# Selective scan with a quantized feed-forward: dt u B of two states and D u by diagonal products on TensorE, state 11's C product on GpSimd

## What is computed

```python
dA = jnp.exp(d[..., None] * A)                              # d is dt, per channel and position
state = state * dA + (d * u)[..., None] * b[:, None, :]     # 16 states per channel
y = jnp.einsum('bdn,bn->bd', state, c)
...
y = (y + D[None, :, None] * x) * silu(z)
...
x = x + jnp.tanh(g_xattn[0]) * xattn(ctx, layernorm(x), ...)
x = x + jnp.tanh(g_ffn[0]) * ffn(layernorm(x), w_gate, w_up, w_down)
```

## Time and profile before

| | |
|---|---|
| median of 3 runs | 623.98 us (623.07 to 625.08) |
| the profiled execution | 624.87 us |
| its span, first to last instruction | 623.1 us |
| mean granted clock of TensorE | 0.970; 1.00 in the windows of units 5 to 15 |

### The profile page before, as it was taken

The page is one execution under the profiler, slowest core; times in us unless marked ns, Lnnn a source line. Parts: engine busy times, 40 slices in busy tenths (PEclk is TensorE's granted clock), DMA queues, the critical chain, the costliest instruction groups (busy, mean ns, idle before and its releaser), DMA issues. The chain is left out here.

```text
span 623.1 us, 9210 instructions
## 1 busy us (share of the span) xinstructions
PE 501.2 (80%) x3014; PEld 338.2 (54%) x3014; DVE 564.6 (91%) x777; ACT 510.7 (82%) x761; POOL 519.9 (83%) x286
## 2 busy tenths in 40 slices
PE   6999666856576788888768888888697978899997
PEld 2443355745575665556555655555465655555553
DVE  2899979999999999999999999999999999987564
ACT  3869789886997898969598989786889898778784
POOL 1568799999999999999999999999999999941000
PEclk9999768789889999999999999999999999999999
DMA  8992941710751010118400111075101010000001
GB/s 284 400 413 80 347 157 34 262 60 1 283 184 40 1 51 2 34 35 312 163 34 35 35 34 35 34 265 207 37 34 35 35 34 19 1 17 18 18 18 50
DMA packets 29985, 64.47 MB, mean 103 GB/s; under 512 B 3681, under 2 KB 11873, under 8 KB 26866
## 3 DMA queue, kind: packets, MB, share of 16 engines
q1 hardware_dynamic: 29938, 63.89, 28.5%
HBM read 55.75 MB, written 8.13 MB: 103 GB/s over the span
## 5 line engine op out<-in xcount | busy, mean ns | idle before, releaser
L759 POOL TENSOR_TENSOR area_s<-area_s,b_bc 128x1024 f32<-128x1024 f32 x128 | 300.6, 2365 | 7.9 <-DMA b_bc<-bc_rows 3.6
L438 PE MATMUL pY<-ident,area_s 128*128 128x128 f32 x640 | 103.2, 287 | 79.7 <-DVE area_s L1329 76.8
L438 PEld LDWEIGHTS pY<-ident,area_s 128*128 128x128 f32 x640 | 73.3, 145 | 108.6 <-DVE area_s L1329 78.9
L1005 ACT ACTIVATE pA<-dt_all,a_neg 128x512 f32<-128x512 f32 x160 | 107.7, 681 | 13.8 <-DVE area_s L1321 12.8
L1321 DVE TENSOR_TENSOR_SCAN area_s<-pA,area_s 128x512 f32<-128x512 f32 x96 | 114.2, 1204 | 4.2 <-ACT pA L1005 3.6
L481 PE MATMUL pG<-wq_gu,area_f 128*128 128x512 fp8e4 x448 | 106.6, 379 | 3.7 <-ACT area_f L955 2.9
L751 POOL TENSOR_TENSOR u_all<-u_all 128x1024 f32<-128x1024 f32 x44 | 104.0, 2363 | 0.2 <-DMA u_all<-bc_rows 0.2
L1329 DVE TENSOR_TENSOR area_s<-area_s,pC 128x512 f32<-128x512 f32 x144 | 95.1, 663 | 2.4 <-DVE area_s L1321 0.7
L432 PE MATMUL pC<-ident,xdT 128*128 128x128 f32 x576 | 90.4, 284 | 3.1 <-DVE area_s L1329 1.9
L432 PEld LDWEIGHTS pC<-ident,xdT 128*128 128x128 f32 x576 | 69.9, 143 | 11.4 <-DVE area_s L1329 8.3
L481 PEld LDWEIGHTS pG<-wq_gu,area_f 128*128 128x128 bf16 x448 | 41.9, 98 | 48.1 <-ACT area_f L955 3.9
(11 more groups left out here) (197 smaller groups left out, 977.7 us busy)
## 6 DMA issues: line engine op xcount, KB each, us to landing
b_bc<-bc_rows SPq DMA_DIRECT2D x16, 1024.0 KB, 8.0
area_s<-x SPq DMA_DIRECT2D x32, 256.0 KB, 3.0
u_all<-bc_rows SPq DMA_DIRECT2D x14, 512.0 KB, 6.2
b_bc<-w_gate SPq DMA_DIRECT2D x1, 4096.0 KB, 14.3
dt_all<-x SPq DMA_DIRECT2D x1, 4096.0 KB, 24.6
area_f<-w_up SPq DMA_DIRECT2D x1, 4096.0 KB, 34.0
area_f<-w_down SPq DMA_DIRECT2D x1, 4096.0 KB, 15.1
out<-area_f SPq DMA_DIRECT2D x16, 256.0 KB, 2.1
```

The lines of the kernel that those rows point to most:

```text
L438: mm = pe.matmul(pY[:, k * P:(k + 1) * P], src[:, k * P:(k + 1) * P], ident[:, :], is_transpose=True, start=(first and k == 0), stop=(last ...
L759: gp.tensor_tensor(db[c % NDB], du[s % 2].rearrange("p (a l) -> p a l", a=1).to_broadcast([P, CH, L]), b_bc[:, CH * c:CH * c + CH, :], ALU ...
L1005: act.activation(exp_bank(s, n), dt_all[:, s, :], ACT.Exp, scale=a_neg[:, s % NT, n:n + 1]).then_inc(S["s_exp"], 1)
```

## The change

From unit 5 on (`PE_FROM`):

- dt u B of states 4 and 5 (`PE_PAIR = 2`) is made by PE instead of POOL. `du_transpose` transposes dt u into pT, ACT copies it to SBUF (`copy_duT`, step 15 of the unit before), and `db_state` multiplies it, as stationary operand, with 128x128 diagonal matrices of B into the PSUM bank that would have held the exponential. The exponential of these two states goes to the SBUF buffer `db[2]` instead, and the scan swaps its operands. The diagonals are made by ACT from `ident` and a column of `xdT`, eight for each batch, in the last unit of the batch before (unit 4 for the first).
- The product of state 11 with C is made by POOL alone (`times_c_alone`, 512 columns, with a row of C broadcast by a DMA), and PE sums it from there (`y_sum_alone`). DVE's product and PE's broadcast of C for this state go.

In all units D u is no longer made on ACT: ACT makes a 128x128 diagonal of D (`diag_d`), and `y_skip` multiplies u with it into pY. In units 0 to 3 it moves to an earlier step. Some small tiles move to tensors of their own. The core of the diff:

```diff
+PE_FROM = PLAIN + 1
+PE_PAIR = 2
+ALONE = 11
+def alone(s, n):
+    return s >= PE_FROM and n == ALONE
 def own(s):
-    return [n for n in range(NS) if n // CH not in pooled(s)]
+    return [n for n in range(NS) if n // CH not in pooled(s) and not alone(s, n)]
+def pool_pairs(s):
+    return [c for c in range(NCH) if s < PE_FROM or c != PE_PAIR]
+DIAGONAL_AT = {3: ((0, 0), (0, 1)), 4: ((0, 2), (0, 3)), 5: ((1, 0),), 6: ((1, 1),), 9: ((1, 2),), 10: ((1, 3),)}
+def by_pe(s, n):
+    return s >= PE_FROM and n // CH == PE_PAIR
...
+        h_alone = carve(area_f, 4096, L)
+        c_alone = carve(area_f, 7680, L)
-        du_skip = carve(area_s, 8192, L)
+        duT = carve(area_s, 8192, L).rearrange("p (k d) -> p k d", k=NT)
+        diag_b = [b_bc[:, CH * PE_PAIR + i, :].rearrange("p (k l) -> p k l", k=NT) for i in range(CH)]
...
             def load_u(s):
                 past(sp, S["s_du"], s - 1)
-                past(sp, S["s_skip"], s - 1)
+                past(sp, S["s_skd"], s - 1)
...
+            def load_c_alone(b):
+                if b == 1:
+                    sp.wait_ge(S["k_p3"], 2 * NW + 1)
+                else:
+                    sp.wait_ge(S["s_amul"], b * NT - PE_FROM)
+                sp.dma_start(c_alone, bc_rows[b, NS + ALONE].partition_broadcast(P)).then_inc(S["d_ca"], 16)
...
+                    first = 4 * q + (CH if b * NT >= PE_FROM and 2 * q == PE_PAIR else 0)
...
+            def y_sum_alone(s):
+                pe.wait_ge(S["s_amul"], s - PE_FROM + 1)
+                y_part(h_alone).then_inc(S["s_aytr"], 1)
...
             def y_skip(s):
                 if s >= PLAIN:
                     pe.wait_ge(S["s_y"], s)
+                past(pe, S[f"d_u{s % 2}"], (s // 2) * 16)
                 pe.wait_ge(S["s_skip"], s + 1)
-                y_part(du_skip, first=(s >= PLAIN)).then_inc(S["s_skd"], 1)
+                for k in range(NT):
+                    mm = pe.matmul(pY[:, k * P:(k + 1) * P], u_in[s % 2][:, k * P:(k + 1) * P], diag_d[:, :],
+                                   start=(s >= PLAIN and k == 0), stop=False, skip_group_check=True)
+                mm.then_inc(S["s_skd"], 1)
+            def du_transpose(s):
+                pe.wait_ge(S["s_du"], s + 1)
+                pe.wait_ge(S["s_szT"], s)
+                for k in range(NT):
+                    mm = pe.transpose(pT[:, k * P:(k + 1) * P], du[s % 2][:, k * P:(k + 1) * P], ident[:, :])
+                mm.then_inc(S["s_dup"], 1)
+            def db_state(s, i):
+                n = CH * PE_PAIR + i
+                pe.wait_ge(S["s_duT"], s - PE_FROM + 1)
+                pe.wait_ge(S["s_diag"], CH * NT * (s // NT - 1) + NT * (i + 1))
+                pe.wait_ge(S["s_scan"], s * NS + n - 2)
+                for k in range(NT):
+                    mm = pe.matmul(exp_bank(s, n)[:, k * P:(k + 1) * P], duT[:, k, :], diag_b[i][:, k, :], start=True, stop=True)
+                mm.then_inc(S["s_dbp"], 1)
...
             def down(t, part, z_done):
...
-                    pe.wait_ge(S["s_szT"], z_done)
+                    if z_done < UNITS:
+                        pe.wait_ge(S["s_duT"], z_done - PE_FROM + 1)
+                    else:
+                        pe.wait_ge(S["s_szT"], z_done)
...
-                    if n == NS - 1:
+                    if n == 10:
                         y_skip(s)
...
             for s in range(PLAIN, UNITS):
                 t1, t2 = s - NT, s - NT - 1
-                fill(s, 0, 1)
+                if s >= PE_FROM:
+                    du_transpose(s)
                 if s > PLAIN:
                     y_sum(s - 1, 15)
                     y_sum_pooled(s - 1, 3)
                 c_bcast(s, 2)
-                fill(s, 1, 2)
+                fill(s, 0, 1)
+                if s >= PE_FROM:
+                    db_state(s, 0)
+                    db_state(s, 1)
                 y_skip(s)
                 y_sum(s, 2)
                 c_bcast(s, 3)
-                fill(s, 2, 4)
+                fill(s, 1, 4)
...
-                    c_bcast(s, 11)
...
-                y_sum(s, 11)
+                if ALONE in own(s):
+                    y_sum(s, ALONE)
...
                     up(t1, 3)
+                    if s >= PE_FROM:
+                        y_sum_alone(s)
                     y_sum(s, 14)
...
+            def times_c_alone(s):
+                gp.wait_ge(S["d_ca"], (s // NT) * 16)
+                gp.wait_ge(S["s_scan"], s * NS + ALONE + 1)
+                gp.tensor_tensor(h_alone, h_alone, c_alone, ALU.mult).then_inc(S["s_amul"], 1)
...
                     times_b(s + 1, 1)
-                    times_b(s + 1, 2)
+                if s >= PE_FROM:
+                    times_c_alone(s)
                 times_c(s, 3)
...
             def exponential(g):
                 s, n = g // NS, g % NS
+                if by_pe(s, n):
+                    act.wait_ge(S["s_scan"], (s - 1) * NS + CH * (PE_PAIR + NDB) + CH)
+                    act.activation(db[PE_PAIR][:, n % CH, :], dt_all[:, s, :], ACT.Exp, scale=a_neg[:, s % NT, n:n + 1]).then_inc(S["s_exp"], 1)
+                    return
...
             def skip(s):
-                past(act, S[f"d_u{s % 2}"], (s // 2) * 16)
                 past(act, S["s_skd"], s)
-                act.activation(du_skip, u_in[s % 2], ACT.Copy, scale=d_raw[:, s % NT:s % NT + 1]).then_inc(S["s_skip"], 1)
+                act.activation(diag_d[:, :], ident[:, :], ACT.Copy, scale=d_raw[:, s % NT:s % NT + 1]).then_inc(S["s_skip"], 1)
+            def copy_duT(s):
+                act.wait_ge(S["s_dup"], s - PE_FROM + 1)
+                past(act, S["s_dbp"], CH * (s - PE_FROM))
+                act.activation(duT.rearrange("p k d -> p (k d)"), pT[:, :], ACT.Copy).then_inc(S["s_duT"], 1)
+            def diagonal(b, i, k):
...
+                n = CH * PE_PAIR + i
+                act.activation(diag_b[i][:, k, :], ident[:, :], ACT.Copy, scale=xdT[:, b, k, n:n + 1]).then_inc(S["s_diag"], 1)
...
+                    if s == PE_FROM - 1 and n in (2, 4, 6, 8):
+                        diagonal(1, n // 6, n - 2 - 4 * (n // 6))
+                        diagonal(1, n // 6, n - 1 - 4 * (n // 6))
+                    if s % NT == NT - 1 and s + 1 < UNITS and n in DIAGONAL_AT:
+                        for i, k in DIAGONAL_AT[n]:
+                            diagonal(s // NT + 1, i, k)
...
                     if n == 14:
                         z_copy(s)
+                    if n == 15 and s + 1 < UNITS:
+                        copy_duT(s + 1)
...
             def scan(s, n):
                 dve.wait_ge(S["s_exp"], s * NS + n + 1)
-                if n % CH == 0:
-                    dve.wait_ge(S["s_dbu"], s * NCH + n // CH + 1)
+                at, dbu = exp_bank(s, n), db[(n // CH) % NDB][:, n % CH, :]
+                if by_pe(s, n):
+                    dve.wait_ge(S["s_dbp"], CH * (s - PE_FROM) + n % CH + 1)
+                    at, dbu = dbu, at
+                elif n % CH == 0:
+                    dve.wait_ge(S["s_dbu"], db_count(s, n // CH))
...
+                elif alone(s, n):
+                    past(dve, S["s_aytr"], s - PE_FROM)
+                    h = h_alone
```

45 lines of the change are left out of this document (30 added, 15 removed).

## The result

| | before | after |
|---|---|---|
| median (runs) | 623.81 us (7, 623.07 to 625.08) | 627.99 us (7, 626.27 to 628.62) |
| the profiled execution | 624.87 us | 627.36 us |
| its span | 623.1 us | 625.5 us |

The changed kernel is slower: the ratio of the two kernels' runs is 1.0061, with a 95% interval of 1.0047 to 1.0075 (the two medians alone give 1.0067). In a later comparison it was 1.0039 (1.0018 to 1.006), with medians of 627.96 us against 624.79.

The account below looks back on a forecast made before the run. VectorE and GpSimd were taken as full, with ScalarE second bound 0.24 us behind VectorE in a loop. Terms 2.75 + 4.5 + 0.45 - 2.8 + 0.3 - 0.2 = +5.0 gave 629.0 us, range 617.5 to 634.

Parts of the forecast that it names:

- Ordinary units: Units 6, 9, 10, 13 and 14: 31.1 us each instead of 30.55, 5 x 0.55 = +2.75 us.
- unit 15: Unit 15, which issues no diagonals: +0.45 us.
- The last stretch: TensorE's last stretch loses one broadcast: -0.2 us.
- TensorE's stretch and ScalarE's chain: TensorE's 2.15 us more per unit delay copy_duT and copy_xqT; quantizing starts at 16.15 after scan 14 instead of 15.46.
- the rival of dear products: Rival, chance 0.10: fp32 products on TensorE cost 0.35 us each, +13, about 642; at 0.25, +3.4, 632.4.
- From `scale_h` to scan 14: ScalarE's quantizing of h through exponential 14: 14.9 us, putting the scan of state 14 at 31.05.
- Diagonals: Units 7 and 11: eight on ScalarE at 0.30 us, two hidden, 1.8 over 31.1 gives 32.9, +2.25 each, +4.5.
- Units 8 and 12: VectorE's 0.79 us wait goes and the saved product of 0.58 counts: 33.5 us, -1.4 each, -2.8.
- Unit 4: Unit 4 holds eight diagonals (2.4 us) among gaps of ScalarE: +0.3 us.
- TensorE fits in: Rival, chance 0.20: copy_xqT waits for ScalarE alone, ordinary units 30.5 us; -1.0 in all, 623.0.
- The relief goes through: Rival, chance 0.25: ScalarE's order has unseen room, VectorE's 0.58 us comes off each of 11 units: -6.4, 617.6.
- The two full engines' own sums: Four units (9 to 12) would need 121.2 us of GpSimd and 121.1 of VectorE, instead of 126.61.

Follow-up runs that it names:

- three moves: The changed kernel with xq's transpose ahead of nine fp8 products, all eight diagonals at step 3, and dt u transposed one unit earlier: 621.67 us, ratio 0.9941.
- the best kernel: The kernel with the three moves plus 11 idle transposes that keep TensorE busy in unit 4: 621.02 us, ratio 0.9922 against before.
- two tries to cut the loop: On the best kernel, VectorE's scales made earlier, with ScalarE's scaling half ahead of exponential 7, or both halves between exponentials 7 and 8: 623.28 and 622.91 us.

## Why the prediction was right, and where its terms were off

The predicted sign and mechanism held: from unit 4 on after is 3.3 us longer where +5.0 was the sum, and the medians differ by 4.2 in the first comparison and 3.2 in the second. Part of the closeness of 627.99 to 629.0 is luck. Ordinary units, unit 15 and units 7 and 11 were priced 3.2 us too high, unit 4 1.1 too low, and the 0.9 us between the units' 3.3 and the medians' 4.2 are not accounted for. (The last stretch, priced at -0.2, did not change: 73.14 and 73.12 us.)

**TensorE's stretch and ScalarE's chain: right to 0.2 us.** Counted from the scan of state 14: `du_transpose` at 4.61 (4.43 foreseen), `squares` 6.35 (6.25), `xq_transpose` 14.42 (14.3), `copy_xqT` 15.06 (14.97), `scale_h` 16.16 (16.15). ScalarE's wait for TensorE there is 0.57 (0.5) and VectorE's idle time ahead of scan 14 is 0.52 (0.5 or more; 0.31 in unit 6, the least). The 0.18 us of `du_transpose` are GpSimd's: its product of state 11, which was to be done at 2.9, ends at 3.18, and TensorE waits 0.30 us for it ahead of `y_sum_alone`:

```profile
366.67 0.66 PE L487 MATMUL pY<-ident,area_f 128*128 128x128 f32 x4 [0.30 <-POOL area_f L855]
```

GpSimd gained idle time as foreseen: ahead of its products for a pair it is 21.9 us over the span, where the earlier trace rows has 7.9. The price of an fp32 product is 0.22 (0.215), so the rival of dear products is out.

**From `scale_h` to scan 14: the term that was too large.** The prediction added 14.9 us. It measured 14.52 (379.59 to 394.11), so an ordinary unit came to 30.69 and not 31.1, +0.13 for +0.55, and five of them to +0.65 for +2.75. The number was read where ScalarE was abreast of VectorE, and contained the 0.34 us of waits for scans. In after, where ScalarE is the late one, they are gone: exponential 14 starts 13.79 us behind `scale_h`, for 14.16 before. The run with more work for ScalarE met the same room: its segment grew by 0.38 where 0.61 was expected. Unit 15 has the same term: +0.03 for +0.45.

**Diagonals: the cost right, the sign not.** One takes 0.295 us (0.30 foreseen). Units 7 and 11 came to 32.43 and 32.70, which is 1.7 and 2.0 over an ordinary unit where 1.8 was the sum. In the run that moved the diagonals into the hole ahead of `copy_xqT`, 1.6 of unit 7's 1.7 us and 1.7 of unit 11's 2.1 went away. But VectorE was to stand idle for over 1.5 us ahead of scan 14 there, and it is 0.79 and 1.06. The time is spread over several waits; in unit 11 the largest is one for TensorE's product of the up projection, just ahead of that scan (0.56 us before):

```profile
425.05 0.69 DVE L1404 TENSOR_TENSOR area_f<-area_f,pG 128x512 f32<-128x512 f32 x1 [1.77 <-PE pG L556]
426.80 1.22 DVE L1452 TENSOR_TENSOR_SCAN area_s<-pA,area_s 128x512 f32<-128x512 f32 x1 [1.06 <-ACT pA L1106]
```

**Units 8 and 12: the right size by a wrong split.** They came to 33.57 for 33.5. The prediction had VectorE's wait of 0.79 for exponential 14 go and VectorE's saved product count. The wait is still 0.79:

```profile
460.37 1.22 DVE L1452 TENSOR_TENSOR_SCAN area_s<-pA,area_s 128x512 f32<-128x512 f32 x1 [0.79 <-ACT pA L1106]
```

ScalarE's wait for the residual, 4.56 us, shrank to 1.15, and behind it stands a new one for VectorE's statistics:

```profile
438.64 0.63 ACT L1028 ACTIVATE w_xp_sb<-dt_all 128x512 f32<-128x512 f32 x1 [1.15 <-POOL dt_all L819]
...
443.28 0.72 ACT L1016 ACTIVATE area_f<-dt_all,mv 128x512 f32<-128x512 f32 x1 [1.30 <-DVE mv L1379]
```

The row of the residual stands 2.5 us earlier against scan 14 than before (11.84 for 14.33), the centring (L1016) only 1.1: it starts at 16.48 behind scan 14 of unit 11, against 17.6 before (440.93 less 423.32), and from there to exponential 14 ScalarE needs 16.4 us for 16.5: 1.1 and 0.2 make the 1.3. That GpSimd's relief brought the earlier residual is argued from its order and not tested apart. The run with product 11 back on VectorE puts the share of that product at 0.44.

**Unit 4: missed.** +1.43 for +0.3. The prediction priced its diagonals and did not ask what the earlier place of D u does to TensorE where there is little other work for it. Two runs narrow it down: with D u by the diagonal alone the whole +1.4 is there, and with TensorE kept busy at full clock 0.9 of it goes. What the other 0.5 us are stays open.

**The rivals.** "TensorE fits in" is out by its own test, the wait of 0.57 at `copy_xqT`. "The relief goes through" did not come about in this kernel, though its reason was sound: ScalarE's order had room, and after three moves the units fell to 30.34, the total to 621.7. It was to decide from under 14.3 us between the scales and the end of exponential 14; that segment has 14.48 in after (379.59 to 394.07), nearer than the 14.85 read before. What held the units was not its length but its late start. The two full engines' own sums (121 us for four units) were not reached: the best kernel needs 124.9. So taking work off the two engines with the highest busy shares did not by itself make the kernel faster.

## What to carry to other kernels

Work moved from a full engine to one with gaps is paid in latency where a third engine waits in order for its result: here 2.15 us more of TensorE between two sums made two of ScalarE's copies late, and putting those two results (and the diagonals) ahead of work that nobody waits for turned +0.6% into -0.6%. When two engines take turns in a loop, measure the length of an engine's segment in a run where that engine is the late one; read where the two are abreast, as here, it can contain waits that the view doesn't name. An engine that starts to lead in a loop gains nothing by starting its step earlier if the buffers that the other frees are on the same turn: here two tries to cut the loop at one place only closed it at a neighbouring exponential.
